# Polynomial attention of an audio tower on one Trainium2 core: from head-wise feature products to computed scores

## The reference

```
h = tokenizer(x)                      # depthwise conv, stride 2 -> (32, 188, 64), norm, PReLU
h = h + alibi_attention(ln(h))        # 8 heads, softmax
h = h + expert_attention(ln(h))       # 4 heads x 4 experts, two small norms and an MLP
h = h + taylor_attention(ln(h))       # the stage that the change rewrites
h = h + mixture(ln(h))                # 8 experts, the best two of each token
```

```
qn = normalize(q * s) * s * temperature;  kn = normalize(k) * s      # s = 8 ** 0.25
vN = concat([1, v]) / 188                                            # 9 columns a head
kv_mod = einsum('bhni,bhnj,bhne->bhije', kn, kn, vN)
kv = einsum('bhnd,bhne->bhde', kn, vN);  vsum = sum(vN over tokens)
y = 0.5 * einsum('bhni,bhnj,bhije->bhne', qn, qn, kv_mod) + s**2 * einsum('bhnd,bhde->bhne', qn, kv) + s**4 * vsum
y = y[..., 1:] / y[..., :1]
out = y @ Wproj.T + bproj
```

## Time and profile before

| | |
|---|---|
| median of 3 runs | 2035.8 us (2035.69 to 2038.83) |
| the profiled execution | 2043.5 us, its span 2041.7 us |
| mean granted TensorE clock | 0.858 of full |
| PE busy | 1719.6 us, 84% of the span |
| DVE busy | 1488.7 us, 73% |
| ACT busy | 755.0 us, 37% |
| POOL busy | 690.7 us, 34% |

### The profile page before, as it was taken

How to read it: one execution, slowest core, us unless ns; L and a number is a source line. 1 busy time by engine, 2 the same in 40 slices (tenths; PEclk the granted TensorE clock), 3 DMA queues, 4 the chain that set the end, 5 groups by cost and what they waited for, 6 DMA issues and landing times. The chain is left out here.

```text
span 2041.7 us, 45613 instructions
## 1 busy us (share of the span) xinstructions
PE 1719.6 (84%) x15064; PEld 1344.5 (66%) x15064; DVE 1488.7 (73%) x4423; ACT 755.0 (37%) x2274; POOL 690.7 (34%) x957
## 2 busy tenths in 40 slices
PE   1499999999689999999999999946999997888990
PEld 1266666666567777777777777735888887777780
DVE  6276766666537888898898988876666664988881
ACT  2254445454234443434343444312222222433440
POOL 2522222222144544555545445432121112222210
PEclk9999999999789999999999999955555555988885
DMA  2000000000000000000000000000000000000001
GB/s 112 1 2 0 0 0 0 0 0 0 1 1 1 2 1 0 0 0 0 0 0 0 0 0 0 1 0 1 0 0 0 0 1 1 1 0 0 0 2 30
DMA packets 6952, 8.13 MB, mean 4 GB/s; under 512 B 6244, under 2 KB 6244, under 8 KB 6756
## 3 DMA queue, kind: packets, MB, share of 16 engines
q1 hardware_dynamic: 6884, 7.25, 1.0%
HBM read 5.71 MB, written 1.54 MB: 4 GB/s over the span
## 5 line engine op out<-in xcount | busy, mean ns | idle before, releaser
L1143 ACT ACTIVATE ex_pT<-ex_T 128x376 f32<-128x376 f32 (+1 forms) x384 | 162.4, 439 | 217.4 <-PE ex_T L1045 208.1
L605 ACT ACTIVATE al_prob<-al_S,al_negmax 94x94 f32<-94x94 f32 (+1 forms) x512 | 146.0, 375 | 180.2 <-DVE al_negmax L732 180.2
L1208 DVE TENSOR_REDUCE ex_negmax<-ex_R 94x2 bf16<-94x376 f32 (+1 forms) x384 | 186.8, 543 | 30.5 <-PE ex_R L1016 30.0
L1045 PE MATMUL ex_T<-ex_qm,ex_kpad 128*128 128x188 f32 x1024 | 189.8, 329 | 0.0
L506 PE MATMUL al_S<-al_kpad,al_qT 128*94 128x376 f32 x384 | 166.5, 516 | 0.0
L1045 PEld LDWEIGHTS ex_T<-ex_qm,ex_kpad 128*128 128x128 f32 x1024 | 163.1, 192 | 5.1
L945 POOL TENSOR_SCALAR_AFFINE_SELECT ex_pT<-ex_pT 128x512 f32<-128x512 f32 x128 | 84.4, 660 | 236.6 <-ACT ex_pT L1143 236.6
L683 POOL TENSOR_TENSOR al_kpad<-al_kT,al_quad_mask 128x1504 f32<-128x1504 f32 x32 | 86.2, 2693 | 186.1 <-ACTq L620 186.1
L732 DVE TENSOR_REDUCE al_negmax<-al_S 94x2 f32<-94x376 f32 (+1 forms) x192 | 99.1, 542 | 62.5 <-PE al_S L507 56.6
L1555 POOL TENSOR_TENSOR ta_kk<-ta_ext 94x320 f32<-94x320 f32 x64 | 60.4, 962 | 246.4 <-DVE ta_qkn L1735 163.0
L1028 PE MATMUL ex_R<-ex_sxT,wsb 128*128 128x188 f32 x256 | 72.2, 364 | 47.5 <-DVE ex_negmax L1208 47.5
(11 more groups left out here) (308 smaller groups left out, 4301.0 us busy)
## 6 DMA issues: line engine op xcount, KB each, us to landing
tok_xin<-x_t SPq DMA_DIRECT2D x4, 760.0 KB, 6.5
wsb<-weights SPq DMA_DIRECT2D x1, 2531.0 KB, 13.9
out<-stream SPq DMA_DIRECT2D x2, 752.0 KB
tok_par<-tok_w SPq DMA_DIRECT2D x1, 4.5 KB, 1.6
```

The lines of the kernel that those rows point to most:

```text
L605: last = nc.scalar.activation(p[:, k, cols], S[0:P, k, cols], ACT.Exp, bias=negmax[g % 2][:, m:m + 1])
L1045: last = nc.tensor.matmul(T[:, k, (j % 2) * N:(j % 2 + 1) * N], kpad[par][:, j, 0:K0], qm[e % 2][:], start=True, stop=True)
L1143: nc.scalar.activation(pT[e % 2][rows, k, cols], T[rows, k, cols], ACT.Exp)\
L1208: red(dst, src, AX.X, ALU.max, negate=True).then_inc(sem["r_used"], 1)
```

## The change

Only the Taylor stage is rewritten, and the two biases move into the weights. The lines named here are those of the changed kernel.

- q and k are scaled into padded tiles, 32 columns a head of which 8 are used (`qkn`, L1708), and both are transposed (L1602), 4 heads side by side on 128 partitions, into the one PSUM bank QK: first q, then, after ACT's copy (L1666), k.
- Scores (L1536): for each group of 4 heads, 8 matmuls of 32 rows each, at four row positions of the array (`tile_position=(32 * j, 0)`), into the four banks of T. T holds one group.
- Weights (L1633): ACT computes (t + s**2)**2 with Square and a bias, 94 x 752 elements an instruction, four a row.
- Weighing (L1548): for each group, 8 matmuls of 32 output columns (`tile_position=(0, 32 * j)`) into O; DVE copies O (L1715).
- The constant s**4 times the sum of vN (L1586) by a matmul with a flat 94x94 matrix, and a matmul with a 0/1 matrix that turns the 9 used rows of each head back to token rows (L1589), both summed in one PSUM region.
- The bias of q, k, v and of the projection becomes a 65th row of the weights, against a row of ones in xT and yT (L1620, L1609). The bias additions go.
- Most tiles have one buffer now, a row is in flight over five turns, not eight. xT, yT, Y and the projection share the one bank X. GpSimd only sets constants.

```diff
-    ("wqkv", 192), ("bqkv", 192), ("wproj", C), ("bproj", C), ("temp", TH),
+    ("wqkv", 192), ("wproj", C), ("temp", TH),
...
+            def scores(r, g):
+                u = G * r + g
+                if g == 0:
+                    pe.wait_ge(qk_ready, 2 * (r + 1))
+                need(pe, t_used, u)
+                for s in range(HALVES):
+                    for j in range(GH):
+                        rows = slice(32 * j, 32 * j + 32)
+                        last = nc.tensor.matmul(T[0:P, j, s * N:(s + 1) * N], kT[rows, g, s * P:(s + 1) * P],
+                                                qT[rows, g, :], start=True, stop=True, tile_position=(32 * j, 0),
+                                                skip_group_check=True)
+                last.then_inc(t_full, 1)
+
+            def weigh(r, p, g):
+                pe.wait_ge(t_used, G * r + g + 1)
...
+                        last = nc.tensor.matmul(O[32 * j:32 * j + 32, g * N:(g + 1) * N], v1[p][:, s, GH * g + j, :],
+                                                prob[g][:, j, s * N:(s + 1) * N], start=(s == 0), stop=(s == 1),
+                                                tile_position=(0, 32 * j), skip_group_check=True)
...
+                if valid(rf):
+                    pe.wait_ge(y_ready, rf + 1)
+                    need(pe, stored, rf)
+                    need(pe, xT_ready, upto(rx + 1))
...
+                    for full, first in ((qT_full, 0), (kT_full, G)):
+                        if first:
+                            pe.wait_ge(qk_ready, 2 * rq + 1)
...
+                if valid(rf):
+                    pe.wait_ge(yT_ready, rf + 1)
+                    need(pe, y_ready, upto(rw + 1))
...
+                ins = nc.scalar.activation(prob[g][:, 2 * k:2 * k + 2, :], T[0:P, 2 * k:2 * k + 2, 0:HALVES * N],
+                                           ACT.Square, bias=linear[:])
```

More of the change, by code:

```diff
@@ L1431, in taylor_attention @@
     nc, stream, w = env["nc"], env["stream"], env["w"]
[L1432 to L1441, removed]
+    ident = env["ident"]
+    GH = 4
+    G = TH // GH
     V1 = TD + 1
+    PAD_D = 32
+    NORMS = HALVES * 2 * TH
     with ExitStack() as ctx:
@@ L1445, in sb, with psum @@
             return ctx.enter_context(nc.sbuf_tensor("ta_" + name, shape, dt))
[L1447 to L1451, removed]
+        def psum(name, shape):
+            return ctx.enter_context(nc.psum_tensor("ta_" + name, shape, F32))
         def sem(name):
@@ L1466, in taylor_attention @@
[L1466 to L1480, removed]
+        xn = sb("xn", [P, HALVES, C])
+        xT = sb("xT", [C + 1, N])
+        squares = sb("squares", [P, HALVES, 128])
+        norm2 = sb("norm2", [P, NORMS])
+        norm = sb("norm", [P, NORMS])
+        least = sb("least", [P, HALVES, 2 * TH])
+        factor_of = sb("factor_of", [P, HALVES, 2 * TH])
+        factor = sb("factor", [P, NORMS])
@@ L1481, in taylor_attention @@
+        qkn = sb("qkn", [P, HALVES, 2 * G, GH * PAD_D])
+        qT = sb("qT", [128, G, N])
+        kT = sb("kT", [128, G, N])
+        v1 = [sb(f"v1_{i}", [P, HALVES, TH, PAD_D]) for i in range(2)]
+        prob = [sb(f"prob{i}", [P, GH, HALVES * N]) for i in range(G)]
+        oT = sb("oT", [128, G * N])
+        pick = sb("pick", [128, GH, V1])
+        flat_part = sb("flat_part", [P, P])
+        linear = sb("linear", [P, 1])
         rec = sb("rec", [P, HALVES, TH])
-        y = two("y", [P, HALVES, TH, TD])
@@ L1501, in valid, with upto, projected @@
             return not isinstance(r, int) or 0 <= r < B
+        def upto(n):
+            return min(n, B) if isinstance(n, int) else n
         def row_halves(r):
             return stream[:, bass.ds(r * HALVES, HALVES), :]
[L1506 to L1510, removed]
+        def projected():
+            return QKV[0:P, 0:HALVES * 192].rearrange("p (h c) -> p h c", h=HALVES)
         @block.gpsimd
@@ L1519, in const @@
                 pool.wait_ge(consts, count[0])
[L1521 to L1535, removed]
+            const(nc.gpsimd.memset(qkn[:], 0.0))
             for t in v1:
-                const(nc.gpsimd.memset(t[:], 1.0 / N))
+                const(nc.gpsimd.memset(t[:], 0.0))
+                const(nc.gpsimd.memset(t[:, :, :, TD:V1], 1.0 / N))
             const(nc.gpsimd.memset(factor_of[:], TS))
@@ L1558, in _ @@
-            skewed_loop(pool, body, DEPTH)
+            const(nc.gpsimd.memset(xT[:], 1.0))
+            const(nc.gpsimd.memset(yT[:], 1.0))
+            const(nc.gpsimd.memset(linear[:], TS2))
+            const(nc.gpsimd.memset(flat_part[:], TS4))
+            const(nc.gpsimd.memset(pick[:], 0.0))
+            const(nc.gpsimd.affine_select(out=pick[:], in_=pick[:], compare_op=ALU.not_equal, fill=1.0, base=0,
+                                          pattern=[[-PAD_D, GH], [-1, V1]], channel_multiplier=1))
@@ L1693, in body @@
             def body(t, par):
[L1694 to L1700 removed]
+                rq, rw, rf = t - 2, t - 4, t - 5
@@ new lines, in body @@
+                if valid(rq):
+                    dve.wait_ge(squares_ready, rq + 1)
+                    need(dve, norm_ready, rq)
+                    nc.vector.tensor_reduce(norm2[:], squares[:].rearrange("p h (a d) -> p (h a) d", d=TD), AX.X, ALU.add)\
+                        .then_inc(norm2_set, 1)
+                if valid(t):
+                    for h in range(HALVES):
+                        last = nc.vector.bn_stats(stats[:, h, :], stream[:, t * HALVES + h, :])
+                    last.then_inc(stats_set, 1)
+                    dve.wait_ge(stats_set, t + 1)
+                    dve.sem_inc(stats_settled, 1)
+                    for h in range(HALVES):
+                        last = nc.vector.bn_aggr(moments[:, h, :], stats[:, h, :])
+                    last.then_inc(var_set, 1)
+                    dve.wait_ge(var_set, t + 1)
+                    nc.vector.tensor_scalar(moments[:, :, 1], moments[:, :, 1], LN_EPS, None, ALU.add)\
+                        .then_inc(moments_ready, 1)
@@ new lines, in body @@
+                if valid(rw):
+                    dve.wait_ge(w_full, G * (rw + 1))
+                    need(dve, y_full, rw)
+                    nc.vector.tensor_copy(oT[:], O[:, 0:G * N]).then_inc(o_ready, 1)
+                if valid(t):
+                    dve.wait_ge(std_ready, t + 1)
+                    nc.vector.reciprocal(rstd[:], std[:]).then_inc(rstd_set, 1)
+                    dve.wait_ge(rstd_set, t + 1)
+                    need(dve, xT_full, t)
+                    for h in range(HALVES):
+                        last = nc.vector.tensor_scalar(xn[:, h, :], stream[:, t * HALVES + h, :], moments[:, h, 0:1],
```

370 lines of the change are left out of this document (146 added, 224 removed).

## The result

The changed kernel takes 2178.5 us (median of 4 runs, 2175.9 to 2181.6) against 2037.3 for the kernel before on the same chip: ratio 1.069, 95% interval 1.066 to 1.072, slower. The forecast was 2175 with half clock throughout as its likeliest case. The profiled execution took 2175.9 us for a span of 2174.2.

The account below looks back on a forecast made before the run. TensorE at half clock bounds the Taylor stage: 12.2 us of work plus shape changes and waits make 14.1 a turn; 33 x 14.1 = 465, +139.8 over 325.5, so 2175 us against the median 2035.8; range 2060 to 2250.

Parts of the forecast that it names:

- Half clock throughout: Taylor stage: TensorE's clock stays at 0.50 for the whole stage, giving 2175 us; chance 0.50.
- Row tiles as cheap as col tiles: Scores groups: four row-tiled matmul records run for the price of one, 1.36 us a group at half clock.
- Rival 3: Scores groups: row tiles do not overlap their weight loads, 16.3 us a turn, 2248 us; chance 0.08.
- Weighing: Col-tiled weighing groups: four sets at 0.34, 1.36 us a group, twice a row.
- Constant part and pick: 8 matmuls a turn, 16 records at 0.153, 2.44 us at half clock.
- Transposes of q and k: Eight transposes a turn with 128 weight columns, 0.21 each, 1.67 us in two halves.
- Waits: TensorE waits on ScalarE's copies: 0.4 us before the yT transposes, 0.75 before the k transposes.
- A square: ScalarE's square of 94x752 from PSUM: 0.88 us, 0.1 less where the next overlaps it.
- Sum: One turn of the new loop: 14.1 us at half clock; the stage 33 x 14.1 = 465 us.
- The factor of 33: Taylor stage: 32 rows last 33.0 turn periods, fill and drain costing about one row; used for the new loop too.
- What lay under TensorE's work: Work removed from VectorE and GpSimd in the Taylor stage is worth nothing, as it lay under PE's work.
- Rival 1: Taylor stage: full clock for most of it, 9.2 us a turn, 2014 us, faster than before; chance 0.15.

Follow-up runs that it names:

- twice: Changed kernel with each scores group computed twice, row-tiled as it is; 2139.3 us, ratio 1.051 to the kernel before.
- whole: Changed kernel with scores on the whole array, no row tiles, all 128 rows contracted; 2211.1 us, ratio 1.086 to the kernel before.
- fill_a2: Changed kernel in the order of reorder, with eight idle matmuls a turn between yT transposes and projection, and bursts; 2064.2 us, ratio 1.014 to the kernel before.
- reorder: Changed kernel, same instructions in another order: scores 1 before yT transposes, q transposes before the constant part; 2161.8 us, ratio 1.060 to the kernel before.
- noflat: Changed kernel without the constant part of the polynomial (four matmuls, 8 records a turn); 2135.2 us, ratio 1.048 to the kernel before.
- fill_a: Changed kernel with six idle whole-array matmuls a turn in three pairs, and bursts; 2160.6 us, ratio 1.056 to the kernel before.
- fill_b2: Kernel before with twelve idle matmuls a turn in pairs at six places, and bursts ahead of the loop; 2005.8 us, ratio 0.984 to the kernel before.
- fill_b3: As fill_b2 with 256-column fillers, 1280 columns a turn moved to the thin part, one burst of 8; 1992.1 us, ratio 0.979 to the kernel before.
- fill_b4: As fill_b3 with 1024 filler columns a turn, none before xT and 128 before qq; 2134.8 us, ratio 1.045 to the kernel before.
- fill_b: Kernel before with six idle matmuls a turn in three pairs, and bursts; 2123.3 us, ratio 1.040 to the kernel before.
- noburst: fill_b2 without its two bursts, nothing else changed; 2013.9 us, ratio 0.987 to the kernel before.

## Why the prediction was right, by its own steps

- **Half clock throughout** (0.50 of the chance): right; 0.50 in every window of the stage. The prediction took it from the nearest stage and called itself far from sure, and the choice was in part lucky: computing the scores twice was enough to move the clock part of the time. It leaned on matmuls that are thin or short. The experiments agree as far as they go: with more in the same scores groups (twice, 0.70 in 1500 to 1540), with whole-array scores (whole, 0.83), or with fillers (fill_a2, 1.00), the clock comes up, and with fewer waits (reorder, 0.50 in 1400 to 1800) it does not. Which property counts, rows, columns, the share of transposes or the length of a dense stretch, no run separates.
- **Row tiles as cheap as col tiles** (1.36, between 1.36 and 5.44): right; 0.31 a set of four (twice) instead of 0.34, and 1.51 - 1.26 = 0.25 left for the change of shape that I priced at 0.1. The two errors nearly cancel. Rival 3 is out.
- **Weighing** 1.36 and a change: 1.41 before QKV. **Constant part and pick** 2.44: measured 2.58, 0.16 a record by noflat. **Transposes of q and k** 1.67: about 0.68 to 0.9 a half, a little less than forecast.
- **Waits** 0.4 and 0.75: measured 0.44 and 0.57 (0.54 and 0.57 in the turn before), released by the two copies named. **A square** 0.88: measured 0.877, and 1.66 for two in a row, so 0.1 overlaps, as taken. The squares start 1.64 after scores 0 (1561.56 to 1563.20), where the forecast had 1.6.
- **Sum**: 14.1 against 14.17 and 14.28 a turn; the stage 465.9 against 465 (33.0 turns of 14.1). No step of the turn is off by more than 0.2, and the misses go both ways. The factor of 33 held for the new loop too, with 32.6 to 32.9.
- **What lay under TensorE's work** was worth nothing, as said: VectorE lost 70 us of work over the stage and GpSimd nearly all of its 60, and no time came of it.
- **Rival 1's price** (9.2 at full clock) was not measured without fillers. By fill_a it is about 9.6, with the late y division that the rival named: the yT transposes start 3.30 after scores 0 where it had 2.95, and the projection 7.73 where it had 7.15. 33 turns of 9.6 would be 2027 us, an estimate, hardly under the kernel before; what failed the rival is its condition. At equal clocks the old form is ahead: 9.86 to 14.2 at half, 8.56 to 10.2 with both filled (twelve fillers in the old, eight in the reordered new).

The fall of the clock that both kernels' stage inherits came with an idle time of TensorE: in the expert stage's tail, where the prediction saw only the busy time of 8.28 of 12, TensorE was idle for 3.99 us; the clock was 1.00 in 1332 to 1335, 0.69 in 1335 to 1336.3 and 0.50 in 1336.3 to 1340. In the kernel before:
```profile
1336.27 1.14 PE L986 MATMUL ex_X<-ident,ex_zn 94*128 94x94 f32 x4 [3.99 <-DVE ex_hx L1232]
```
An idle time like that does not explain what follows. The Taylor stage's turns shown have no idle above 0.57 us, TensorE is busy for 37.12 of 40, and the clock stays at 0.50; and in twice it falls within a turn whose longest idle time is 0.85. What makes the clock rise or fall is not shown.

## What to carry to other kernels

Price a new loop at both levels of the clock, and read from the nearest stage of the same kernel which it will get; busy time was no guide to that: thin matmuls kept TensorE busy for 38.16 of 40 us at 0.50, and fill_a2 stood at 1.00 with 36.10. Where a stage bound by TensorE stands at 0.50, try idle whole-array matmuls between its thin ones before restructuring it: here they gave the old form 2.1%, but with a fifth fewer columns the same idea cost it 4.5%. And work that lay in TensorE's shadow gained nothing by leaving: the new form took 70 us of work off VectorE, which was not waited for, and put 120 us of busy time on TensorE, which was.

## What the runs showed of the hardware that was not expected

- More work made a kernel faster: 1024 more records of scores, 39 us less (2178.5 to 2139.3); the granted clock in 1500 to 1540 was 0.70 where it had been 0.50.
- Four records in a row to one row tile did not hold up the other tiles: 1.60 a group, interleaved 1.58.
- In the old form 1536 columns of fillers a turn in six places held the clock at 1.00 (fill_b2), and 1280 moved towards the thin stretch did too (fill_b3); 1024 did not (fill_b4), nor did 768 in three places (fill_b). Number and place were changed together, so these runs do not tell which of them counts. In the new form, reordered, 1024 were enough (fill_a2). Why the level is kept or lost within a turn is not settled beyond that.
- noburst: at half clock the pairs alone still brought the clock up, between 1420 and 1430 us, after more than 20 us with TensorE busy without a break at 0.50.
